# Second mean aggregation: the x2 rows are added on TensorE, and the sums are read from PSUM

## The reference, cut to what matters

```python
def _mean_aggr(x, src, dst, n):
    s = jax.ops.segment_sum(x[src], dst, num_segments=n)
    cnt = jax.ops.segment_sum(jnp.ones((src.shape[0],), x.dtype), dst, num_segments=n)
    return s / jnp.maximum(cnt, 1.0)[:, None]

def _sage(x, src, dst, Wl, b, Wr):
    m = _mean_aggr(x, src, dst, x.shape[0])
    return m @ Wl.T + b + x @ Wr.T

h = jax.nn.relu(_sage(x2, src, dst, W1l, b1, W1r))     # first aggregation
x3 = _layernorm(x2 + _sage(h, src, dst, W2l, b2, W2r)) # second aggregation
```

## Time and profile before

| | us |
|---|---|
| median of 3 runs | 2895.54 (2893.41 to 2901.38) |
| profiled execution | 2897.93 |
| its span, first to last instruction | 2896.2 |
| busy over the span: VectorE | 2309.7 (80%) |
| TensorE | 1832.9 (63%) |
| ScalarE | 1740.0 (60%) |
| GpSimd | 1695.7 (59%) |
| granted clock of TensorE, mean | 0.814 |

### The profile page before, as it was taken

How to read it: one execution, slowest core, us unless ns; L and a number is a source line. 1 busy time by engine, 2 the same in 40 slices (tenths; PEclk the granted TensorE clock), 3 DMA queues, 4 the chain that set the end, 5 groups by cost and what they waited for, 6 DMA issues and landing times. The chain is left out here.

```text
span 2896.2 us, 51835 instructions
## 1 busy us (share of the span) xinstructions
PE 1832.9 (63%) x9687; PEld 1401.4 (48%) x9687; DVE 2309.7 (80%) x9110; ACT 1740.0 (60%) x4457; POOL 1695.7 (59%) x1605
## 2 busy tenths in 40 slices
PE   5666666456656653777777666657775666657663
PEld 4655555344545542554455333335664555534442
DVE  7887777798988874788888688857886989888883
ACT  3444445323222233888888688865555888858885
POOL 7777777346666664333333556637775766327675
PEclk8777777688788875899999899988998888757776
DMA  6777767534444435999999789967886888734441
GB/s 179 238 242 229 241 222 234 168 72 79 85 76 79 76 47 171 335 341 345 351 344 347 256 290 300 303 219 235 259 256 206 295 291 292 266 129 166 158 165 52
DMA packets 280171, 625.34 MB, mean 216 GB/s; under 512 B 51230, under 2 KB 84649, under 8 KB 280055
## 3 DMA queue, kind: packets, MB, share of 16 engines
q1 hardware_dynamic: 207543, 523.73, 53.0%
q0 software_dynamic: 72512, 100.52, 15.7%
HBM read 342.76 MB, written 285.23 MB: 217 GB/s over the span
## 5 line engine op out<-in xcount | busy, mean ns | idle before, releaser
L1249 ACT ACTIVATE node_out<-node_in,n_shift,n_root 128x128 f32<-128x128 f32 (+1 forms) x1176 | 468.1, 482 | 80.3 <-DVE n_shift L1563 80.1
L786 POOL DMA_INDIRECT sums<-gat_sums,dst_safe_i x196 | 185.3, 946 | 293.7 <-DVE pre L1979 237.7
L903 POOL DMA_INDIRECT out_dram<-node_x2t,out_index x196 | 209.3, 1068 | 160.0 <-ACT node_x2t L1450 93.7
L794 POOL DMA_INDIRECT src_rows<-x_table,row_i x200 | 201.0, 1005 | 130.6 <-issue 53.8
L786 POOL DMA_INDIRECT src_rows<-in_x_dram,src_i x196 | 195.7, 999 | 84.4 <-issue 83.0
L794 POOL DMA_INDIRECT sums<-x_table,row_i x192 | 192.7, 1004 | 85.9 <-issue 50.0
L849 POOL DMA_INDIRECT gat_sums<-src_rows,add_idx x100 | 160.2, 1602 | 138.6 <-ACT src_rows L1321 45.8
L1546 DVE BATCH_NORM_STATS2 n_stats<-node_in 128x6 f32<-128x256 f32 (+1 forms) x588 | 209.4, 419 | 22.6 <-DMA node_in<-y_nodes 11.6
L1026 PE MATMUL ps<-alpha,node_in 128*128 128x196 f32 x392 | 111.5, 447 | 179.1 <-DVE junk L1869 175.8
L794 POOL DMA_INDIRECT own_rows<-in_x_dram,dst_safe_i x196 | 189.8, 968 | 59.7 <-issue 56.4
L1258 ACT ACTIVATE t_a<-ps 128x512 f32<-128x512 f32 (+1 forms) x198 | 115.9, 585 | 158.8 <-PE ps L948 158.6
(11 more groups left out here) (414 smaller groups left out, 6614.0 us busy)
## 6 DMA issues: line engine op xcount, KB each, us to landing
own_rows<-x_table SPq DMA_DIRECT2D x245, 256.0 KB
node_in<-in_x_dram SPq DMA_DIRECT2D x96, 512.0 KB
x_table<-node_out SPq DMA_DIRECT2D x96, 512.0 KB
x_table<-new_rows SPq DMA_DIRECT2D x147, 256.0 KB
gat_sums<-node_x2t SPq DMA_DIRECT2D x49, 528.0 KB, 4.0
acc_dump<-acc SPq DMA_DIRECT2D x98, 264.0 KB
node_sums<-gat_sums SPq DMA_DIRECT2D x48, 528.0 KB
h_table<-node_h SPq DMA_DIRECT2D x48, 512.0 KB
```

The costliest lines, as they stand in the source:

```text
L786: g_.indirect_dma_start(out=to[:, g.b, j, 0:width], out_offset=None, in_=tab, in_offset=bass.IndirectOffsetOnAxis(ap=indices(j), axis=0)). ...
L794: g_.indirect_dma_start(out=to4[g.q][:, j, 0:F], out_offset=None, in_=tab, in_offset=bass.IndirectOffsetOnAxis(ap=indices(j), axis=0)).the ...
L903: g_.indirect_dma_start(out=out[:, :], out_offset=bass.IndirectOffsetOnAxis(ap=out_index[:, t:t + 1], axis=0), in_=wide_new[:, g.b, j, :], ...
L1249: last = sc.activation(to[0:pn, g.b, j, :], rows[0:pn, g.b, j, 0:F], ACT.Identity, bias=NORM[k][2][0:pn, g.b, j:j + 1], scale=root[0:pn, j ...
```

## The change

The addition of the own x2 rows moves from VectorE to TensorE: a product of the identity with the x2 rows is accumulated into the bank of `sage_out`. The buffer `pre` and its signal go. VectorE's statistics and ScalarE's `new_x3` read the bank itself, which is therefore in use until `new_x3` has written the rows (`newd`). The bias product and the product with the identity stand ahead of the waits for the two copies, and behind a wait for `newd` of step g - 2. SP's load of the x2 rows waits for the products (`mm`) of step g - 2.

```diff
-            x2_own = load_own(L, L["pre"], x2_table, own2_rows, L["own2"])
+            x2_own = load_own(L, L["mm"], x2_table, own2_rows, L["own2"])
...
             def sage_out(g, jn=J):
+                wait_free(pe, L["newd"], g)
+                if g is not FIX:
+                    wait_landed(pe, L["own2"], g)
+                own = fix_own[:, 1, :] if g is FIX else own2_rows[:, g.b, :, :].rearrange("p j f -> p (j f)")
+                te.matmul(ps[3][g.b][:, 0:jn * F], ones_bf[:, :], b2_parts[:, 0:jn, :].rearrange("p j f -> p (j f)"),
+                          start=True, stop=False)
+                te.matmul(ps[3][g.b][:, 0:jn * F], ident[:, :], own, start=False, stop=False)
                 wait_done(pe, L["cp_a"], g)
                 wait_done(pe, L["cp_b"], g)
-                wait_free(pe, L["pre"], g)
-                te.matmul(ps[3][g.b][:, 0:jn * F], ones_bf[:, :], b2_parts[:, 0:jn, :].rearrange("p j f -> p (j f)"),
-                          start=True, stop=False)
...
-            new_x3, root = normed_rows(L, "e", pre, new_rows, "newd", "stored"), roots(L, "e")
+            root = roots(L, "e")
+
+            def new_x3(g, jn=J):
+                wait_drained(act, L["stored"], g)
+                wait_done(act, L["e_nm"], g)
+                for j in range(jn):
+                    last = sc.activation(new_rows[:, g.b, j, :], ps[3][g.b][:, j * F:(j + 1) * F], ACT.Identity,
+                                         bias=NORM["e"][2][:, g.b, j:j + 1], scale=NORM["e"][1][:, g.b, j:j + 1])
+                last.then_inc(L["newd"].sem, 1)
...
-            def x3_sums(g, jn=J):
-                if g is not FIX:
-                    wait_landed(dve, L["own2"], g)
-                own = fix_own[:, 1, :] if g is FIX else own2_rows[:, g.b, :, :].rearrange("p j f -> p (j f)")
+            def x3_moments(g, jn=J):
                 wait_done(dve, L["mm"], g)
-                wait_free(dve, L["newd"], g)
-                v.tensor_tensor(pre[:, g.b, 0:jn, :].rearrange("p j f -> p (j f)"), ps[3][g.b][:, 0:jn * F],
-                                own, ALU.add).then_inc(L["pre"].sem, 1)
-
-            def x3_moments(g, jn=J):
-                wait_done(dve, L["pre"], g)
-                moments((L, "e", g, pre, P, jn))
+                wait_free(dve, L["e_nm"], g)
+                for j in range(0, jn, 2):
+                    last = v.bn_stats(NORM["e"][0][:, g.b, j:j + 2, :].rearrange("p j c -> p (j c)"),
+                                      ps[3][g.b][:, j * F:(j + 2) * F].rearrange("p (j f) -> p f j", f=F))
+                last.then_inc(L["e_bn"].sem, 1)
+                variances(L, "e", g, P, jn, NORM["e"][1][:, g.b, :])
...
-            pipeline(dve, STEPS, edges((3, x3_shifts), (0, sources_landed), run[0], (2, x3_sums), run[1], (2, x3_moments), run[2], run[3],
+            pipeline(dve, STEPS, edges((3, x3_shifts), (0, sources_landed), run[0], run[1], (2, x3_moments), run[2], run[3],
                                        (0, means)), per=4)
```

More of the change, by code:

```diff
@@ L468, in gnn_program @@
             "nodes3": dict(front=norm("n") + ["n_row"], rings=dict(n_in=1, n_out=1), steps=DENSE_STEPS),
-            "sage2": dict(back=["accd", "rcp", "msgd", "tr_a", "cp_a", "tr_b", "cp_b", "mm", "pre", "newd", "e_cn"] + norm("e"),
+            "sage2": dict(back=["accd", "rcp", "msgd", "tr_a", "cp_a", "tr_b", "cp_b", "mm", "newd", "e_cn"] + norm("e"),
                           rings=dict(own=1, own2=1, dumped=1, stored=1), quads=dict(quad=J)),
@@ L2102, in _ @@
             means(FIX, 1)
-            x3_sums(FIX, 1)
             x3_moments(FIX, 1)
```

## The result

The changed kernel takes 3005.33 us, the median of four runs (2997.67 to 3017.09); the kernel before took 2897.22 beside it (four runs, 2893.41 to 2901.38). The ratio is 1.0376, 95% interval 1.0338 to 1.0415: slower, and 1.7 us from the forecast of 3007. The profiled execution took 3008.05 us with a span of 3006.3, that is 110.1 more than the span before.

A forecast was written before the change was run, and what follows sets the result against it. It took a TensorE-ScalarE ring in the second aggregation, at a mixed clock, as the bound: 45 x (7.56 - 5.12) = 110, plus 1.39 for the turn before, +111 us, 3007 against 2895.5. Range 2960 to 3045.

The forecast's parts named there:

- The wait: Second mean aggregation: `sage_out` waits for ScalarE's rows, queued behind copies; 1.39 us added per turn, bounds 0 and 1.53.
- The product: TensorE's identity product stands behind the same wait, hidden by nothing: 0.91 us at upper clock, 1.87 at lower.
- The turn: One TensorE and ScalarE step of the second aggregation: 6.54 us at upper clock, 10.15 at lower, mean 7.56.
- The clock: TensorE's granted clock in the second aggregation falls from 0.92 to 0.81, with 0.28 of turns slow.
- What was costed at nothing: Second aggregation: PSUM statistics, x2-row loads, dump and store, gathers, and the tail after the last `sage_out` add nothing.
- The turn ahead of the 45: Turn before the 45 counted ones, waiting for the fourth gather as before: takes only the added 1.39 us.
- The first: Same queue dependence in the second aggregation, clock nearly always lower: +228 us, 3123; chance 0.09.
- The second: VectorE's dropped addition counts, if ScalarE's rows end before the copies: 5 us faster, 2890; chance 0.05.
- the third rival: No change: gathers, one every 1.25 us, hold the second aggregation at 5 us a step; 2895; chance 0.04.
- the same ring: Second aggregation: copies of g, rows of g-2, `sage_out(g)`, transposes and copies of g+1 in line; shortest turn 6.54 us.

The follow-up runs named there:

- the first experiment: Kernel before with one edit: products of step g wait for `newd` instead of `pre`, no identity product; 2983.18 us, ratio 1.0293.
- the product alone: Changed kernel's identity product, but VectorE still copies the bank into `pre` and TensorE waits for `pre`; 2894.9 us, ratio 0.9982 against the kernel before.

## Why the prediction came out right

**The wait.** The step that decided, the signal `newd` in place of `pre`, is shown by itself: +84 us from one word. TensorE's pause is the 2.3 us that were worked out, and the rows take 1.51 us where 1.5 was taken. From the end of the second copy (2104.77 + 0.59 = 2105.36) to the bias product it is 1.53 us where 0.24 + 1.39 = 1.63 was worked out, since the product follows the rows' end by 0.13 and not by 0.24.

**The product.** 0.91 us was forecast for the upper clock; the turns with and without it differ by 0.85. For the lower clock it was 1.87: the slow turn shows just that, 1.87 from 2097.85 to 2099.72, yet the slow turns with and without it differ by 1.3 only (9.5 and 8.18), as the second transposes are at the upper clock again here (0.61 us) and are not there (1.06). TensorE of the kernel after, in order of time:

```profile
2097.32 0.60 PE L1146 MATMUL ps<-b_parts,ones_bf 3*128 3x512 bf16 x1 [2.28 <-ACT new_rows L1405]
2097.85 2.08 PE L1148 MATMUL ps<-own_rows,ident 128*128 128x512 f32 x2
2099.72 0.63 PE L1153 MATMUL ps<-w2l_t,t_a 128*128 128x128 f32 x2
...
2103.13 1.03 PE L948 MATMUL ps<-ident,msg 128*128 128x128 f32 x4
2103.99 0.61 PE L948 MATMUL ps<-ident,own_rows 128*128 128x128 f32 x4
```

**The turn.** At the upper clock 6.54 was forecast and 6.38 came. At the lower, 10.15 was forecast and 9.57 is the longest seen. Most of the difference is that no turn stays low to its end: the first transposes above take 1.03 us, the second, alike, 0.61. The same turn in two parts, in the table of stretches:

```profile
2097.30:2103.20 5.90, 5.88 (x20) 4.41 (x21) 1.35 (x6) 0.00 (x0) 2.90 (x4) 0.50 0.42 132
2103.20:2106.80 3.60, 1.40 (x9) 1.16 (x7) 2.83 (x10) 2.52 (x7) 0.94 (x1) 0.89 0.63 196
```

So both sizes were put too high. The forecast had 0.28 of the turns slow to their end and the rest without the lower clock; instead 25 of 45 meet it for a part. In the mean, 7.66 us against 7.56, these errors nearly cancel.

**The clock.** 0.81 was taken from the stage with the same busy share of TensorE, and 0.81 was granted. The value was right, but the way to it was not sound. The share of 0.63 was that of a turn at the upper clock (4.09 of 6.38 us came, 0.64), and it was set beside a stage whose 0.63 holds at a mixed clock; the edited stage has 265.82 of 390 us, 0.68. Nor does the busy share order the clock in these runs: the wait alone has TensorE busy 181.66 of 279 us, 0.65, and was granted 0.73, and the earlier trace rows has 188.13, 0.67, at 0.89. By that reading I expected too little of the first experiment. So it is in part luck that the clock came out right.

The 45 pauses are alike, 2.2 to 2.3 us, and the bursts behind them are not: 11 begin at the lower clock (0.60 us for the bias product, as at 2097.32), 14 begin at the upper and have lost it by the identity's product (0.38, then 1.90, as at 2106.89 and 2107.20), and 20 run at the upper from end to end. The Trainium skill ("TensorE: Matmul & The Clock Gate", section "HAM oscillation — how this bites in real kernels") tells of a loop whose wait in each turn is longer than the matmuls of the turn, and in which every burst starts cold, that is, at the lower clock. Here the pause is the shorter of the two (2.3 us against 4.09 and more), so that loop is not this one; even so, 11 bursts of 45 start as it says. What decides between the three kinds, no run here tells.

**What was costed at nothing.** Statistics from PSUM take 424 ns (419 from SBUF). The loads of x2 rows show up in none of TensorE's long waits. The turn ahead of the 45 was to add 1.4: step 3's bias product stands 1.5 us earlier than in the earlier trace rows instead. Of these, 1.0 is from earlier stages (the first gather is issued at 1937.00, before at 1938.01), and from that gather to step 3's bias product it is 31.1 us where it was 31.6. So this term wasn't there. The sum: 344.55 - 230.38 = +114.2 for the 45 turns, -1.5 ahead of them and -2.6 behind make the 110.1 of the span. The forecast had 110, 1.4 and 0 for the three. That the total came within 1.7 us, less than the four runs differ among themselves, is in part luck too.

**The rivals.** The first (nearly always at the lower clock) is out: 9.5 us in a quarter of the turns. The second, VectorE's saving, needed ScalarE's rows ahead of the copies; made so, the kernel takes 2891.03, about the 2890 put on it. That the saving does it is not shown: the product alone, in which VectorE saves nothing (210.83 us busy, 212.50 in the earlier trace rows), takes 2894.9. With four gathers the gathers then hold the step, so the third rival's mechanism is true as well, one layer down.

## What to carry to other kernels

When an edit takes out a staging copy, look at which signal frees the double-buffered bank afterwards, and where in its engine's queue that signal's instruction stands: if it stands behind work that needs the waiting engine's next output, the two queues form a ring and work that lay side by side falls into line. Mend it by the order of the queues or by more banks before judging the edit: here the first turned 3.8% slower into 0.23% faster, and the second into a time that can't be told from the one before. Read what an open ring can gain from what holds the step next, by taking that away too.

## What was not expected of the hardware

Work without a use made the kernel faster: with 1.24 us of filler products in the pause of each turn the granted clock rose from 0.81 to 0.94 over the stage, and to 1.00 over the 45 turns, and 3005 us became 2960. The reverse showed too: the same ring without the identity's product was granted 0.73, not 0.81. So the product adds 0.85 us to a turn at the upper clock, 1.3 to a slow one (8.18 to 9.5), and yet only 0.81 in the mean, because fewer turns begin at the lower clock with it, 11 of 45 against 17. And the clock changes regularly: a series of 13 turns that begins at 2063.80, with turns of 6.4, 8.0 and 9.5 us, comes back in the same order from 2162.78 on, with the same pause of 2.3 us ahead of each.
